# A decoder's middle stage: two programs side by side, segment attention in row bands beside wide attention and gate

## The reference

```
h  = norm(x + down(quantised h))                      # after gate and up products of 352 columns
q, k, v = h Wq, h Wk, h Wv                            # 16 heads of 8 features
local   = softmax(q k' / sqrt(8)) v                   # within each segment of 64 tokens, 4 segments
dilated = for every segment: softmax over each 4th token of one segment, weighted by how near it is
h  = norm(h + (local + weighted sum of dilated) Wo)
w  = softmax(mask + (h Wq)(c Wk)' ) (c Wv)            # 16 heads of 64 features on 64 context words
h  = norm(h + w Wout)
gates = softmax(h Wgate)                              # 8 experts, used by the routing that follows
```

## Time and profile before

| | |
|---|---|
| median of three runs | 3885.42 us (3883.22 to 3886.32) |
| the profiled execution | 3881.35 us |
| its span | 3879.4 us |
| busy in the span | PE 69%, PEld 47%, DVE 47%, ACT 29%, POOL 13% |
| mean granted clock of PE | 0.822 of full speed |

### The profile page before, as it was taken

The page is one execution under the profiler, slowest core; times in us unless marked ns, Lnnn a source line. Parts: engine busy times, 40 slices in busy tenths (PEclk is TensorE's granted clock), DMA queues, the critical chain, the costliest instruction groups (busy, mean ns, idle before and its releaser), DMA issues.

```text
span 3879.4 us, 49861 instructions
## 1 busy us (share of the span) xinstructions
PE 2682.1 (69%) x19270; PEld 1804.0 (47%) x19270; DVE 1807.2 (47%) x4261; ACT 1141.7 (29%) x1665; POOL 491.2 (13%) x687
## 2 busy tenths in 40 slices
PE   4554476766767677376895767866688666966678
PEld 3333254544554455244794444444444444444444
DVE  4446655555545555622104654156532655136541
ACT  3342433223323323011002233222432224332332
POOL 0101111111111111054001100010001100011000
PEclk8776587887888798587657799987998889987999
DMA  1000000000000000212220000000000000000000
GB/s 71 0 0 0 0 1 6 6 5 0 6 6 0 6 6 0 81 29 55 71 86 31 1 1 1 1 1 1 1 1 1 1 1 1 1 1 1 1 1 22
DMA packets 41505, 48.69 MB, mean 13 GB/s; under 512 B 6714, under 2 KB 39746, under 8 KB 40580
## 3 DMA queue, kind: packets, MB, share of 16 engines
q1 hardware_dynamic: 35716, 42.25, 3.3%
q0 software_dynamic: 5632, 4.33, 0.9%
HBM read 37.83 MB, written 8.72 MB: 12 GB/s over the span
## 4 chain that ended last, share of the span: by engine, by line
issue 53%; PE 26%; DVE 10%; POOL 8%; ACT 1%; DMA 1%; POOLq 0%; SPq 0%; DVEq 0%; ACTq 0%
PE banks L2287 6%; PE banks L1393 4%; POOL weights L271 3%; DVE weights L2021 2%; PE banks L2276 2%; PE banks L1312 1%; PE banks L1314 1%; PE banks L1313 1%; PE banks L1128 1%; PE banks L1440 1%; PE banks L2224 1%; DVE xs L1422 1%; POOL dilvals L1431 1%; PE banks L1139 1%; DVE dilvals L1414 1%
## 5 line engine op out<-in xcount | busy, mean ns | idle before, releaser
L148 PE MATMUL banks<-wA,weights 128*128 128x128 f32 x768 | 132.2, 327 | 151.5 <-POOL weights L271 144.3
L1414 DVE BATCH_NORM_STATS2 stats<-banks 128x6 f32<-128x128 f32 x192 | 42.8, 286 | 356.3 <-PE banks L1393 297.2
L271 POOL TENSOR_TENSOR weights<-weights,smalls 128x1024 f32<-128x1024 f32 x64 | 122.7, 1917 | 616.6 <-DVE smalls L237 325.2
L182 ACT ACTIVATE weights<-weights 128x1024 f32<-128x1024 f32 x96 | 101.5, 1057 | 331.8 <-DVE weights L225 331.4
L148 PEld LDWEIGHTS banks<-wA,weights 128*128 128x128 f32 x768 | 102.7, 166 | 202.9 <-POOL weights L271 175.0
L2192 DVE TENSOR_REDUCE wide_area<-banks 128x8 f32<-128x2048 f32 x64 | 146.7, 2291 | 107.8 <-PE banks L2112 107.8
L1429 POOL TENSOR_TENSOR rstd<-moments,eps 128x4 f32<-128x4 f32 x48 | 9.6, 201 | 1407.3 <-DVE moments L1418 1407.3
L2164 ACT ACTIVATE weights<-banks 128x2048 f32<-128x2048 f32 x64 | 120.1, 1877 | 121.4 <-PE banks L2125 121.4
L221 DVE TENSOR_REDUCE smalls<-banks 128x16 f32<-128x1024 f32 (+1 forms) x96 | 116.1, 1209 | 53.7 <-PE banks L773 24.4
L1440 PE MATMUL banks<-wA,xs 128*128 128x128 f32 x192 | 50.2, 364 | 115.5 <-DVE xs L1422 114.9
L190 ACT ACTIVATE weights<-banks 128x512 f32<-128x512 f32 x192 | 106.3, 589 | 55.9 <-PE banks L148 54.5
(11 more groups left out here) (736 smaller groups left out, 6747.6 us busy)
## 6 DMA issues: line engine op xcount, KB each, us to landing
big<-long_kernel SPq DMA_DIRECT2D x16, 1024.0 KB, 5.4
big<-in_wE SPq DMA_DIRECT2D x1, 4096.0 KB, 13.3
wC<-in_wC SPq DMA_DIRECT2D x1, 3012.0 KB, 17.2
wC<-in_wG SPq DMA_DIRECT2D x1, 2971.0 KB, 19.7
big<-in_wT SPq DMA_DIRECT2D x1, 2816.0 KB, 10.3
x_all<-in_xT SPq DMA_DIRECT2D x1, 2048.0 KB, 10.5
rows<-xs SPq DMA_DIRECT2D x8, 256.0 KB
total<-xs SPq DMA_DIRECT2D x8, 256.0 KB
```

Of the source, the lines that this page charges most:

```text
L148: mm = pe.transpose(m.PT[:, half, c * P:(c + 1) * P], m.prob[u % 2][:, col:col + P], m.ident)
L271: pool.tensor_tensor(prob, prob, m.rsum[u % 2][:, 0:self.groups].unsqueeze(2).broadcast_to([P, self.groups, self.keys]), ALU.mult).then_in ...
L1414: dve.bn_stats(m.stats[:, i, :], self.tokens(i)).then_inc(*sg.up("dve", f"stats{i}"))
```

## The change

Core, Norm, SegmentLayer, WideLayer and Gate go. Two lanes with four banks each take their place. Near: LaneDown, the norm of the woven stages (LaneNorm, L1398), LaneSegment and a norm again. Far: LaneWide, norm and LaneGate. The loop runs near for group it and far for group it - 1, woven tick by tick with no lag; near for the first group stands ahead of the loop, far for the last behind it. LaneSegment works on one sequence (256 queries) at a time in row bands, as LaneCross does; its local scores have one product for each segment, its dilated values come out with queries on the partitions in blocks of eight segment slots, are divided, weighted and written apart by DVE, and are summed on PE through the unit matrix. LaneWide keeps the unit of 128 queries and 1024 columns, with one pair of banks for scores, one bank for transposes, DVE for the multiplication that POOL had, and the residual added as a product on PE. keep_warm is no longer called. The masks come by two small transfers per group, a pack of constants wY is loaded after the first stage, and the context mask of the last stage later than before.

```diff
+class LaneDown:
...
+    def pe(self, pe, n, x_ready):
+        m, sg = self.lane, self.sig
+        pe.wait_ge(*x_ready)
+        pe.wait_ge(*sg.done("dve", "q3", n))
+        for c in range(CH):
+            r = min(P, INNER - c * P)
+            mm = pe.matmul(m.bank[:, 0, :], m.whole[0:r, QG + c, :], m.whole_h[0:r, c, :], start=(c == 0), stop=(c == CH - 1))
+        mm.then_inc(*sg.up("pe", "product"))
+        yield
+        pe.wait_ge(*sg.done("dve", "resid", n))
+        for i in range(NT):
+            mm = pe.transpose(m.bank[:, 3, i * P:(i + 1) * P], m.resid[:, i * P:(i + 1) * P], m.ident)
+        mm.then_inc(*sg.up("pe", "z"))
+        yield
...
+class LaneSegment:
...
+        for b in range(G):
+            if b:
+                pe.wait_ge(*sg.done("dve", f"norm{b - 1}", n))
+            else:
+                pe.wait_ge(*sg.done("act", "v1", n))
+                pe.wait_ge(*sg.done("dve", f"vd{G - 1}", n))
+                m.carry_product(pe, bank)
+            for i in range(2):
+                for r in range(4):
+                    rows = slice(32 * r, 32 * r + 32)
+                    for s in range(2):
+                        at = b * S + (2 * i + s) * SEG
+                        mm = pe.matmul(bank[SEG * s:SEG * s + SEG, r, i * S:(i + 1) * S], m.qf[rows, at:at + SEG],
+                                       self.local_keys(b, 2 * i + s)[rows, :], start=True, stop=True)
+            mm.then_inc(*sg.up("pe", f"scores{b}"))
+            yield
+            pe.wait_ge(*sg.done("dve", f"max1_{b}", n))
+            self.peaks(pe, f"peaks{b}")
+            yield
+            pe.wait_ge(*sg.done("dve", f"query1_{b}", n))
+            for p in range(2):
+                for g in range(SEGS):
+                    for r in range(4):
+                        rows = slice(32 * r, 32 * r + 32)
+                        mm = pe.matmul(bank[:, r, p * S + g * SEG:p * S + (g + 1) * SEG],
+                                       self.local_keys(b, g)[rows, p * P:(p + 1) * P],
+                                       m.query[rows, p, g * SEG:(g + 1) * SEG], start=True, stop=True)
+            mm.then_inc(*sg.up("pe", f"turned{b}"))
+            yield
+            pe.wait_ge(*sg.done("act", f"exp{b}", n))
...
+            pe.wait_ge(*sg.done("act", f"dil_exp{b}", n))
+            for i in range(2):
+                for c in range(8):
+                    mm = pe.matmul(bank[:, 2 * i + c // 4, c % 4 * self.BLOCK:(c % 4 + 1) * self.BLOCK],
+                                   m.weights[:, c * S + i * P:c * S + (i + 1) * P],
+                                   m.dilvals[:, b, c * self.BLOCK:(c + 1) * self.BLOCK], start=True, stop=True)
+            mm.then_inc(*sg.up("pe", f"dil_out{b}"))
+            yield
+            pe.wait_ge(*sg.done("dve", f"dil_part3_{b}", n))
+            for i in range(2):
+                out = bank[:, 0, i * P:(i + 1) * P]
+                pe.matmul(out, m.heads[:, 2 * b + i, :], m.ident, start=True, stop=False)
+                for g in range(SEGS):
+                    mm = pe.matmul(out, m.parts[:, i, g, :], m.ident, start=False, stop=(g == SEGS - 1))
+            mm.then_inc(*sg.up("pe", f"dil_sum{b}"))
+            yield
+        pe.wait_ge(*biased_ready)
+        pe.wait_ge(*sg.done("act", f"middle{G - 1}", n))
+        summed(pe, bank[:, 3, :], ((m.resid, m.ident), (m.af, w["o"]))).then_inc(*sg.up("pe", "z"))
...
+class LaneWide:
...
+        for u in range(NT):
+            pe.wait_ge(*sg.done("dve", f"mul{u}", n))
+            for half, name in enumerate(("first", "second")):
+                if half:
+                    pe.wait_ge(*sg.done("act", f"copy0_{u}", n))
+                elif u:
+                    pe.wait_ge(*sg.done("act", f"copy1_{u - 1}", n))
+                for c in range(4 * half, 4 * half + 4):
+                    mm = pe.transpose(bank[:, 2, c % 4 * P:(c % 4 + 1) * P], m.prob[u % 2][:, c * P:(c + 1) * P], m.ident)
+                mm.then_inc(*sg.up("pe", f"{name}{u}"))
+            yield
+            pe.wait_ge(*sg.done("act", f"copy1_{u}", n))
+            out = bank[:, 3, u * P:(u + 1) * P]
+            pe.matmul(out, m.resid[:, u * P:(u + 1) * P], m.ident, start=True, stop=False)
+            for c in range(8):
+                mm = pe.matmul(out, m.probT[c // 4][:, c % 4 * P:(c % 4 + 1) * P], m.wide_o[:, u // 2, c, :],
+                               start=False, stop=(c == 7))
+            mm.then_inc(*sg.up("pe", f"out{u}"))
+            if u + 2 < NT:
+                pe.wait_ge(*sg.done("dve", f"sub{u + 1}", n))
+                scores(u + 2)
+            yield
...
+        exp(0)
+        yield from idle(2)
+        for u in range(NT):
+            if u:
+                act.wait_ge(*sg.done("pe", f"out{u - 1}", n))
+            for half, name in enumerate(("first", "second")):
+                act.wait_ge(*sg.done("pe", f"{name}{u}", n))
+                act.activation(m.probT[half], bank[:, 2, :], ACT.Copy).then_inc(*sg.up("act", f"copy{half}_{u}"))
+            if u + 1 < NT:
+                exp(u + 1)
+            yield from idle(2)
...
+        for u in range(NT):
+            prob = m.prob[u % 2].rearrange("p (g k) -> p g k", k=KV)
+            dve.wait_ge(*sg.done("act", f"exp{u}", n))
+            dve.tensor_reduce(m.rsum, prob, AX, ALU.add).then_inc(*sg.up("dve", f"sum{u}"))
+            dve.wait_ge(*sg.done("dve", f"sum{u}", n))
+            dve.reciprocal(m.rsum, m.rsum).then_inc(*sg.up("dve", f"recip{u}"))
+            dve.wait_ge(*sg.done("dve", f"recip{u}", n))
+            dve.tensor_tensor(prob, prob, spread(m.rsum), ALU.mult).then_inc(*sg.up("dve", f"mul{u}"))
+            yield
+            if u + 1 < NT:
+                soft(u + 1)
+            yield
+        yield
...
+        def near_pool(pool, it):
+            if not isinstance(it, int):
+                pool.wait_ge(*far_wide.sig.done("pool", "xf", it - 1))
+                m.carry(pool)
+            pool.tensor_copy(near.xf[:, :], group(m.x_all, it)).then_inc(*near_group.up("pool", "xf"))
...
+        def near_dve(dve, it):
+            yield from near_down.dve(dve, it, m.big[:, :, bass.ds(it * T, T)])
+            yield from near_norm[0].dve(dve, it, near_down.z_ready(it))
+            yield from near_segment.dve(dve, it)
+            yield from near_norm[1].dve(dve, it, near_segment.z_ready(it))
...
+        def far_dve(dve, it):
+            yield from far_wide.dve(dve, it)
+            dve.wait_ge(saved, it * 48 + 16)
+            yield from far_norm.dve(dve, it, far_wide.z_ready(it))
+            yield from far_gate.dve(dve, it)
+        def near_and_far(engine, ahead, behind):
+            for _ in ahead(engine, 0):
+                pass
+            with engine.Fori(1, ITERS) as it:
+                weave(ahead(engine, it), behind(engine, it - 1), middle_ticks, 0)
+            for _ in behind(engine, ITERS - 1):
+                pass
...
+            hscale.pool(pool)
+            pool.wait_ge(*const.done("pool", "segs", 0))
+            pool.memset(far.qmask, 1.0).then_inc(*const.up("pool", "qones"))
+            pool.memset(far.kmask, -far.big).then_inc(*const.up("pool", "kones"))
             for g in range(G * SEGS):
-                pool.tensor_copy(m.segvals[:, g, :].rearrange("p (c j e) -> p c j e", j=2, e=9)[:, :, :, 8],
+                pool.tensor_copy(near.segvals[:, g, :].rearrange("p (c j e) -> p c j e", j=2, e=9)[:, :, :, 8],
...
-            with pe.Fori(0, ITERS) as it:
-                down.pe(pe, it)
-                norm.pe(pe, it * NC)
-                segment.pe(pe, it, norm.sig.done("act", "out", it * NC))
-                norm.pe(pe, it * NC + 1)
-                wide.pe(pe, it, norm.sig.done("act", "out", it * NC + 1))
-                norm.pe(pe, it * NC + 2)
-                gate.pe(pe, it, norm.sig.done("act", "out", it * NC + 2))
+            near_and_far(pe, near_pe, far_pe)
...
+            dve.wait_ge(*const.done("pool", f"seg{G * SEGS - 1}", 0))
+            dve.wait_ge(saved, 16)
+            dve.memset(near.peaks_all, 0.0).then_inc(*const.up("dve", "peaks"))
+            dve.scalar_tensor_tensor(out=near.local_bias, in0=w["head4y"], scalar=col["l1_bk"], in1=w["spare4y"],
+                                     op0=ALU.mult, op1=ALU.subtract).then_inc(*const.up("dve", "local_bias"))
...
+            near_and_far(dve, near_dve, far_dve)
             dve.wait_ge(loaded["wD"], 16)
-            dve.wait_ge(*grp_c.done("pool", "gates", ITERS - 1))
+            dve.wait_ge(*far_gate.sig.done("pool", "save", ITERS - 1))
```

More of the change, by code:

```diff
@@ L866 @@
+NEAR = SEG // DIL
+PAIRS = 8
+EXPERTS = 8
 TILES = TOK // P
@@ L2557, in decoder @@
             lane.peaks = lane.peaks_all.rearrange("p (a i c) -> p a i c", a=2, i=2)
+        near, far = Memory(), Memory()
+        for i, lane in enumerate((near, far)):
+            lane.bank, lane.ident, lane.half2, lane.eps4, lane.minus_half = m.banks[i], m.ident, m.half2, m.eps4, m.minus_half
```

(4 more changed lines are left out.)

1050 lines of the change are left out of this document (493 added, 557 removed), and 1 row of the table WEIGHTS.

## The result

The kernel after takes 4003.47 us (median of four executions, 3999.92 to 4022.11), against 3885.87 us for the kernel before beside it. The ratio is 1.0308, with a 95% interval of 1.0271 to 1.0344: 3% slower, where 1.1% faster was forecast. The profiled execution spans 4001.7 us, that of before 3879.4.

What follows compares the result with a forecast made beforehand. The stage was taken as bound by the order of steps within a group, not by an engine. 2.6 + 90.0 + 7 x 129.8 + 61.7 + 0.9 = 1063.8 us against 1107.4 gave 3842 us; range 3787 to 3912.

Steps and rivals of the forecast that it cites:

- near alone: The near lane for one group with nothing woven beside it: 90.0 us, 10 us longer than in the kernel before.
- (3): Near's local attention: two units of 12.6 us each, with turned scores taken as 2.0 us, 25.2 us together.
- (4): Near's dilated attention: two units of 18.3 us each, with output products taken as 3.8 us, 36.6 us together.
- From there 18.5 + 18.5 + 7.3: Period's tail from 85.5 us: two dilated units, then output product and norm, almost unwoven, ending a period of 129.8 us.
- rival A: TensorE's clock stays low in near's unpaired tail; half of it slow gives period 139 us, kernel 3912 us; chance 0.18.
- two arguments against A: Against a slow tail clock: today's stretch began with a 4.07 us pause, longer than the tail's; dilated values run 3.8 us unbroken.
- The layout: Both lanes' steps laid on the engine queues by their durations, from near's previous output on, giving a period of 129.8 us.
- Far alone: Wide attention and gate with nothing woven beside them: 61.7 us, plus 0.9 for the routing's wait for a copy.
- Rival B: TensorE pauses 0.16 us at some 30 more array-mode changes: period 134.6, 3875 us, sign turned scores over 3 us; chance 0.12.
- no gap: Reading of the earlier trace where TensorE goes from 128-row to 64-row weights: no pause seen, so nothing was put in.
- Rival C: Full overlap: each pair of woven ticks takes only the longer one's time, period some 105 us, 3668 us; chance 0.10.
- no overlap at all: Dismissed case: far waits for near's output at each iteration's head, so the lanes never overlap; no chance given.

Runs made afterwards that it cites:

- tail_sized: Kernel after, with unread identity products added in TensorE's waits in dilated units and the last norm, sized to end before the waits do: 3911.9 us, ratio 1.0057.

## Why the prediction was wrong

**The step that failed** is the length of near alone, (3) and (4), and with it "From there 18.5 + 18.5 + 7.3". The TensorE terms of both units were taken from stretches at the high clock, the first stage's woven units, at 0.97, and the gate's products, for a stretch in which nearly nothing is woven. The nearest row for that stretch stood in the same group: today's dilated stretch, in which TensorE also pauses between short steps (1.6 to 4.1 us), at 0.62. It was given to rival A with a chance of 0.18, and to half the tail. tail_sized shows the sum to be right for the high clock (44.1 for 44.3 us), and the kernel after shows the clock to be the lower one. Of the two arguments against A, neither held. That today's stretch begins with a pause of 4.07 us is no difference, for the tail has none and is as slow. That the dilated values are an unbroken burst of 3.8 us does not help: they run at the low clock for 7.1.

**The account of a period**, in us from near's output to near's next, forecast against the usual iteration of after (timeline, 1020.05 on) and the shortest one of tail_sized behind a jump (1108.7 on; the mean there is 138.2). The layout reaches far's first scores at 32.3, and TensorE does those 2.8 us ahead of near's projections:

| point | forecast | after | tail_sized |
|---|---|---|---|
| near's projections begin | 35.1 | 37.0 | 37.3 |
| first local unit done | 66.8 | 69.4 | 69.7 |
| second local unit done | 83.6 | 90.5 | 90.8 |
| dilated attention begins | 85.5 | 92.2 | 92.5 |
| second dilated unit begins | 104.0 | 116.8 | 111.1 |
| near's output | 129.8 | 150.2 | 136.6 |

Of 20.4 us, 13.7 are the tail's clock. 1.9 are the head: far's first product comes 1.7 us later than without the jump and its first eight products take 6.7 for 5.2, while the steps behind them take 1.3 less than was laid down. The first local unit loses 0.7; the second loses 4.3, of it 1.7 on turned scores at the low clock (3.69 for 2.01), and 1.5 on far's outputs beside them (1.92 and 1.74 for 1.06 each).

**Near alone**: 113.3 for 90.0. The two dilated units give 14.0 us more (50.6 for 36.6), the two local ones 8.2 (33.4 for 25.2), nearly all of it on TensorE's steps. Down projection, norm and projections took 21.7 for 20.9, the output product and last norm 7.5 for 7.3. In (4) the terms as written add up to 18.95 us, not 18.3: the 9.2 up to the exponential fit only with the longer turned scores of a local unit, and the steps of the earlier trace rows give 8.3, with which 18.3 is right; 18.2 was measured at the high clock. VectorE's keys and values, 5.7 us by the forecast, took 5.4:

```profile
472.76 2.96 DVE L1155 TENSOR_SCALAR keys<-banks,wA 128x512 f32<-128x512 f32 x4 [4.58 <-PE banks L1009]
475.64 1.12 DVE L1160 SCALAR_TENSOR_TENSOR spread<-banks,wA 128x128 f32<-128x128 f32 x4
476.68 1.28 DVE L1165 TENSOR_TENSOR wC<-banks,wA 128x512 f32<-128x512 f32 x2
```

**Far alone**: 70.1 for 62.6. The 61.7 do not follow from their terms: with three steps of 6.4 from unit to unit these give about 58. Measured, the first transposes come at 31.2 us for 28.4, the units behind follow 8.0, 7.6 and 6.7 apart, and from the last unit's transposes to the end it is 16.6 us for about 10.

**Rival A** named the mechanism and its sign. By its own price for the whole tail at the low clock, 18 us, the period would have been 148; with half of it, 139, it fell short. The sign that it named, a tail clock near 0.62 and dilated units over 22 us, is what the profile shows. **Rival B** had the price of a change right and their number wrong; its other sign, turned scores of over 3 us, did come, from the clock and not from the array's mode. The reading of the earlier trace rows as "no gap" was wrong: it held the next start against the group's own duration. The same group in front of products that keep the mode (timeline of before) shows the gap:

```profile
931.53 1.97 PE L148 MATMUL banks<-wA,weights 128*128 128x128 f32 x8 [2.75 <-POOL weights L271]
933.29 0.64 PE L160 MATMUL banks<-wA,outT 128*128 128x128 f32 x2
```

The next group starts after 1.76 us here and after 1.89 where the mode changes, 0.13 us later. **Rival C** is out by a period of 150.6, and no overlap at all by 184.3 for the lanes unwoven. "Neither engine is the bound" held: in the usual iteration TensorE is booked for 105.6 of 150.2 us and VectorE for 64.

So the weaving brought what it was to bring, 34 us a period where 22 were forecast; it was paid for with lanes that are longer than forecast, above all near's chains without a partner, in which TensorE stands still between short steps and runs mostly at half its clock. That the removed steps were on the path before was not tried by itself.

## What to carry to other kernels

Before a TensorE duration is moved from one stretch to another, compare the granted clock of the two stretches; where the clock in the target is not known, sum the chain at both levels, and take the lower one for a chain in which TensorE stands still between short steps. When two lanes of unequal length are woven, put the surplus where TensorE has least to do: here moving the pairing by ten ticks was worth 3%. Products that nobody reads can hold the clock; they pay if they end before the wait does and do not stand in front of work behind a jump.

## What the runs showed of the hardware

- Products of the identity in the waits raise TensorE's clock from 0.50 to 1.00 in a dilated unit of this tail, also where they leave waits of 0.2 to 0.7 us (tail_sized).
- A change between products with weights of 128 and of 64 or 32 rows costs 0.19 us at the full clock. A stretch that changes between 128 and 32 rows at each product lost its clock some 5.5 us in (1.00 to 0.51) while its busy share was full.
- 64 passes of 64 columns with 32 rows of weights, in four bands, take 2.01 us at the high and 3.69 us at the low clock; 32 passes of 72 columns with full weights 3.69 and 7.10.
- TensorE's jump back to the head of a loop delayed its next product by 1.7 us here, and with 30 ready products at the head it stood for 3.5 us before the first two and 2.5 us behind them.
